# Row sums of two head pairs in four column tiles, a later normalisation and projection, and four PSUM banks at both ends

## What is computed

```
x = x + 0.5 * ffn(layernorm(x))
x = x + attention_block(layernorm(x))
x = x + 0.5 * ffn(layernorm(x))
```

```
attn = softmax(q k^T / 8)
y = (attn v) w_proj + b_proj + z
y = (y - mean) / sqrt(var + 1e-6) * gamma + beta
```

## Time and profile before

| what | value |
|---|---|
| median of 3 runs | 2347.0 us (2346.77 to 2348.1) |
| the profiled execution | 2348.62 us |
| its span, first to last instruction | 2346.8 us |
| TensorE busy | 2217.9 us, 95% |
| VectorE busy | 1670.9 us, 71% |
| ScalarE busy | 1194.5 us, 51% |
| GpSimd busy | 1470.6 us, 63% |
| mean granted TensorE clock | 0.98 of full speed |

### The profile page before, as it was taken

One profiled execution on the slowest core, in us unless ns is written; L12 is line 12 of the kernel. 1 busy time (PEld: TensorE's weight loads), 2 busy tenths in 40 slices (PEclk: granted clock), 3 DMA queues, 4 the chain that ended last, 5 costly groups with the idle time before them and its releaser, 6 DMA issues.

```text
span 2346.8 us, 38775 instructions
## 1 busy us (share of the span) xinstructions
PE 2217.9 (95%) x14537; PEld 1120.2 (48%) x14537; DVE 1670.9 (71%) x2734; ACT 1194.5 (51%) x1813; POOL 1470.6 (63%) x1419
## 2 busy tenths in 40 slices
PE   3799999999999999999999999999999999999983
PEld 1344445545454554545555454555545454454541
DVE  4465778777787777778777777877777787776643
ACT  1345554545555465555546555554555555454531
POOL 2266666766676675667667576766757676575642
PEclk9799999999999999999999999999999999999985
DMA  1000000000000000000000000000000000000000
GB/s 53 5 7 2 2 7 2 11 2 11 2 7 7 2 11 2 11 2 7 6 2 11 2 11 2 7 7 2 11 2 11 2 6 6 2 7 2 7 2 9
DMA packets 167495, 15.85 MB, mean 7 GB/s; under 512 B 148304, under 2 KB 166928, under 8 KB 167312
## 3 DMA queue, kind: packets, MB, share of 16 engines
q1 hardware_dynamic: 167312, 13.39, 4.9%
HBM read 7.03 MB, written 4.19 MB: 5 GB/s over the span
## 4 chain that ended last, share of the span: by engine, by line
PE 82%; DVE 12%; issue 4%; POOL 1%; ACT 1%; DMA 0%; SPq 0%; POOLq 0%
PE pS L920 21%; PE pO L947 18%; PE pM L904 9%; PE pX L932 6%; PE pX L968 5%; PE pM L1066 5%; DVE nmax L769 3%; PE pM L957 3%; PE FpF L248 2%; PE LpF L283 2%; PE FpF L283 2%; PE LpF L259 2%; PE LpF L248 2%; PE FpF L259 2%; DVE ON L863 1%
## 5 line engine op out<-in xcount | busy, mean ns | idle before, releaser
L634 POOL TENSOR_TENSOR ES<-ES,E 128x512 f32<-128x512 f32 x512 | 701.2, 1390 | 212.6 <-ACT E L721 210.2
L721 ACT ACTIVATE E<-pS 128x1024 f32<-128x1024 f32 x512 | 522.9, 1021 | 411.9 <-PE pS L920 407.6
L769 DVE TENSOR_REDUCE nmax<-pX 128x2 fp32r<-128x1024 f32 x512 | 621.9, 1215 | 129.3 <-PE pX L932 126.4
L947 PE MATMUL pO<-E,VA 128*64 128x512 f32 x2048 | 552.3, 618 | 0.0
L628 POOL TENSOR_TENSOR ES<-E 128x512 f32<-128x512 f32 x256 | 321.4, 1276 | 260.9 <-ACT E L721 260.6
L904 PE MATMUL pM<-xf,w_raw 128*64 128x512 f32 x1024 | 266.1, 598 | 3.1 <-DVE QL L872 2.4
L932 PE MATMUL pX<-KH,QH 64*128 64x512 f32 x1024 | 249.5, 426 | 7.7 <-DVE nmax L769 5.0
L920 PE MATMUL pS<-QH,KH 64*128 64x512 f32 x1024 | 255.5, 496 | 0.0
L920 PEld LDWEIGHTS pS<-QH,KH 64*128 64x128 f32 x1024 | 95.4, 183 | 253.3 <-issue 252.0
L932 PEld LDWEIGHTS pX<-KH,QH 64*128 64x128 f32 x1024 | 189.7, 306 | 51.3 <-DVE nmax L769 12.4
L920 PE MATMUL pS<-SH,onesr 64*128 64x512 f32 x1024 | 203.3, 393 | 0.0
(11 more groups left out here) (135 smaller groups left out, 3291.2 us busy)
## 6 DMA issues: line engine op xcount, KB each, us to landing
RROW<-RC SPq DMA_DIRECT2D x512, 2.0 KB, 2.0
xin<-in_L_attn_x SPq DMA_DIRECT2D x16, 256.0 KB, 3.0
SH<-nmax SPq DMA_DIRECT2D x256, 2.0 KB, 2.0
LC<-LROW SPq DMA_DIRECT2D x256, 2.0 KB, 2.1
out<-X SPq DMA_DIRECT2D x16, 256.0 KB, 2.5
w_raw<-in_L_attn_w_q SPq DMA_DIRECT2D x1, 512.0 KB, 4.7
w_raw<-in_L_attn_w_k SPq DMA_DIRECT2D x1, 512.0 KB, 5.5
w_raw<-in_L_attn_w_v SPq DMA_DIRECT2D x1, 512.0 KB, 6.7
```

The lines of the kernel that those rows point to most:

```text
L634: ins = g.tensor_tensor(ES[par][:, hd, :], ES[par][:, hd, :], E[s][:, hd, :], ALU.add)
L721: a.activation(E[s][:, :, :], pS[:, :, :], ACT.Exp).then_inc(s_exp, 1)
L769: v.tensor_reduce(nmax[px % 2][:, :, t:t + 1], pX[:, :, :], AX.X, ALU.max, negate=True).then_inc(s_max, 1)
L947: ins = pe_.matmul(pO[half(hd), :], VA[of][:, kt, j * 128 + 64 * hd:j * 128 + 64 * hd + 64], E[kt][:, hd, :], start=kt == 0, stop=kt == KT ...
```

## The change

1. Row sums. They are made for two pairs at once, at step 2 of every second pair, at the end of that step on TensorE: four groups of matmuls with 32 columns of ones each, into the four quarters of the partitions of `pM`. `ES` gets a third buffer. `LROW`, `LC`, `REC`, `RC` and `RROW` each carry two pairs: one copy, four DMAs, one reciprocal, two small operations and eight DMAs for two pairs.
2. The broadcast and `ON` come for pair `i-3`, the projection for pair `i-4`.
3. The pieces of `L` move: transposes of x 28, gate 29 to 0, up 1 to 4, transposes of h 10, 11, 13, 14, down 15; on VectorE maxima of h in 4 and 6, rounding of h in 8 and 11, moments of y in 14 and of x2 in 18, maxima of x in 22, rounding of x in 26. `X1` gets three and `X2` two buffers. The pieces of `F` stay, but for one addition on GpSimd (L571), from step 23 to step 25.
4. Both ends. For block 0 of `F` and block 15 of `L` the four row tiles use four banks (`pF`, `pO`, `pM` and half of `pS`), so that a gate needn't wait for the one before it. The first layer norm and quantisation of x stand beside the quantisation of the weights, before the loop, and the loop starts at block -1. Two of the first rounds of V move to block -1, the third to block 0. For block 15 the multiplication by gamma and the addition behind it are on VectorE.

```diff
+    def apart(self, c):
+        return c == self.alone
+    def bank(self, c, k):
+        return self.spare[k] if self.apart(c) else self.pF
...
         if k == 0:
             pe.wait_ge(self.s_xqT, c + 1)
-        else:
+        elif not self.apart(c):
             pe.wait_ge(self.s_silu, 4 * c + k)
...
-        for b in range(-2, B + 2):
+        for b in range(-1, B + 2):
...
-                    if there(i - 2, NP):
-                        sp.wait_ge(s_rlo, i - 1)
-                        for hl in range(2):
-                            for hd in range(2):
-                                sp.dma_start(RROW[2 * hl + hd:2 * hl + hd + 1, :].bitcast(F32),
-                                             RC[old][:, hl, hd, :].bitcast(F32)).then_inc(s_rrow, 16)
+                    if p % 2 == 1 and there(i - 2, NP):
+                        sp.wait_ge(s_rlo, i // 2)
+                        for j in range(4):
+                            for hl in range(2):
+                                r = 4 * hl + j
+                                sp.dma_start(RROW[r:r + 1, :].bitcast(F32), RC[:, hl, j, :].bitcast(F32)).then_inc(s_rrow, 16)
...
-                        if t == 15:
+                        if t == 18:
                             dve.wait_ge(s_x2, c + 1)
-                            norm_x2.moments(nc, dve, c, X2)
-                        if t == 19:
+                            norm_x2.moments(nc, dve, c, X2[c % 2])
+                        if t == 22:
                             dve.wait_ge(norm_x2.s_out, c + 1)
                             L.dve_max_x(dve, c)
-                        if t == 22:
+                        if t == 26:
                             L.dve_round_x(dve, c)
...
-                        if s == 3 and there(i - 2, NP):
-                            dve.wait_ge(s_rb, i - 1)
-                            wait(dve, s_proj, i - 2)
-                            v.tensor_tensor(ON[:, :], OT[(p - 2) % 4][:, :], pM[:, :], ALU.mult).then_inc(s_norm, 1)
+                        if s == 3 and there(i - 3, NP):
+                            dve.wait_ge(s_rb, i - 2)
+                            wait(dve, s_proj, i - 3)
+                            v.tensor_tensor(ON[:, :], OT[(p - 3) % 4][:, :], pM[:, :], ALU.mult).then_inc(s_norm, 1)
...
-                def row_sums(i, par):
-
-                    pe.wait_ge(s_add, 3 * i + 3)
-                    wait(pe, s_norm, i - 1)
-                    pe.wait_ge(s_klo, min(i + 4, NP) if isinstance(i, int) else i + 4)
-                    for hd in range(2):
-                        ins = pe_.matmul(pM[half(hd), :], ones[:, 0:64], ES[par][:, hd, :], start=True, stop=True)
+                def row_sums(i):
+
+                    pe.wait_ge(s_add, 3 * i)
+                    wait(pe, s_norm, min(i - 3, NP))
+                    pe.wait_ge(s_klo, min(i + 3, NP))
+                    for j in range(2):
+                        for hd in range(2):
+                            r = 32 * (2 * j + hd)
+                            ins = pe_.matmul(pM[r:r + 32, :], ones[:, 0:32], ES[(i - 2 + j) % 3][:, hd, :], start=True, stop=True)
                     ins.then_inc(s_l, 1)
...
-                        if s == 2 and there(i - 1, NP):
-                            row_sums(i - 1, 1 - p % 2)
                         first_ffn(b, 4 * p + s, bpar)
                         last_ffn(b, 4 * p + s, bpar)
-                        if s == 1 and there(i - 3, NP):
+                        if s == 1 and there(i - 4, NP):
                             project(i, p)
+                        if s == 2 and p % 2 == 0 and there(i - 1, NP):
+                            row_sums(i)
```

More of the change, by code:

```diff
@@ L419, in make_program @@
         E = [m.sb(f"E{kt}", [128, 2, S]) for kt in range(KT)]
-        ES = [m.sb(f"ES{i}", [128, 2, S]) for i in range(2)]
+        ES = [m.sb(f"ES{i}", [128, 2, S]) for i in range(3)]
         OT = [m.sb(f"OT{i}", [128, S]) for i in range(4)]
@@ L525, in body @@
                                          nmax[new][:, hd, :].bitcast(F32)).then_inc(s_sh, 16)
-                    if p == 4 and there(b + 2, B) and there(b + 1, B):
+                    if p == 4 and there(b + 2, B):
                         sp.wait_ge(s_x1, b + 2)
[L528 to L531, removed]
-                        for hd in range(2):
-                            sp.dma_start(LC[new][:, hd, :], LROW[64 * hd:64 * hd + 1, :]).then_inc(s_lc, 16)
+                        sp.dma_start(tiles(xin[:, :]), x_g[b + 2]).then_inc(s_x, 16)
+                    if p == 4 and there(b - 2, B):
+                        sp.wait_ge(s_res, b - 1)
+                        sp.dma_start(out_g[b - 2], tiles(X2[b % 2][:, :])).then_inc(s_out, 16)
+                    if p % 2 == 0 and there(i - 1, NP):
+                        sp.wait_ge(s_lrow, i // 2)
+                        for j in range(4):
+                            sp.dma_start(LC[:, j, :], LROW[32 * j:32 * j + 1, :]).then_inc(s_lc, 16)
                 steps(sp, body)
@@ L1023, in body @@
                             scores(i, p, s)
-                        if s == 3 and there(i - 2, NP):
-                            pe.wait_ge(s_rrow, 64 * (i - 1))
-                            pe.wait_ge(s_lrow, min(i, NP) if isinstance(i, int) else i)
-                            wait(pe, s_norm, i - 2)
-                            pe_.matmul(pM[:, :], sel[0:64, :], RROW[0:64, :], start=True, stop=True).then_inc(s_rb, 1)
+                        if s == 3 and there(i - 3, NP):
+                            pe.wait_ge(s_rrow, 128 * ((i - 1) // 2))
+                            pe.wait_ge(s_lrow, min(i, NP) // 2)
+                            pe.wait_ge(s_klo, min(i + 3, NP))
+                            wait(pe, s_norm, i - 3)
+                            pe_.matmul(pM[:, :], sel[0:64, (i - 3) % 2, :], RROW[0:64, :], start=True, stop=True).then_inc(s_rb, 1)
                         if s < 2:
@@ new lines, in body @@
+                        if s == 2 and p % 2 == 0 and there(i - 1, NP):
+                            row_sums(i)
+                        for r in rounds_at(i, s):
+                            kt, of, xb = round_place(i, p, bpar, r)
+                            pe.wait_ge(s_klo, min(i + 3, NP))
+                            wait(pe, s_va, r)
+                            if there(i - 3, NP):
+                                pe.wait_ge(s_norm, i - 2)
+                            elif i == 2:
+                                pe.wait_ge(s_lrow, 1)
+                            if p == 5:
+                                pe.wait_ge(s_xf, b + 2)
+                            for n in range(2):
+                                ins = pe_.matmul(pM[half(n), :], xf[xb][:, kt * 128 + 64 * n:kt * 128 + 64 * n + 64],
+                                                 w_raw[:, 2, of * S:of * S + S], start=True, stop=True)
+                            ins.then_inc(s_v, 1)
```

298 lines of the change are left out of this document (150 added, 148 removed).

## The result

The change made the kernel slower: median 2422.1 us (2420.9 to 2423.3) against 2347.6 us (2346.8 to 2350.4) for the kernel before on the same chip, ratio 1.0315 with an interval of 1.0299 to 1.0332. The forecast was 2360 with a range of 2300 to 2405: the sign is right, the size is wrong by 62 us, and the time lies outside the range. The profiled execution took 2423.3 us, its span is 2421.4 us.

What follows compares the result with a forecast made beforehand. TensorE was taken to bound the middle 14 blocks. From the profiled 2348.6 us, row sums -46.7, moved pieces +84, start -19 and end -4 gave 2363, or 2361 against the median; the forecast was 2360, range 2300 to 2405.

Steps and rivals of the forecast that it cites:

- row sums: TensorE's sums: 64 fewer at 0.86 us, less 8.3 us for changes of matmul form; 46.7 us less.
- step 26 to 27: Both roundings of x in step 26 delay ON; step 27's V round stalls 2.3 us in 13 blocks, 30 us.
- step 18 to 19: Moments of x1 and x2 ahead of ON; step 19's V round stalls 2.4 us in 14 blocks, 34 us.
- step 22 to 23: L's maxima of x in step 22 delay ON; the V round stalls 1.0 us in 14 blocks, 14 us.
- steps 7 to 12: VectorE's maxima and roundings of h for F and L: 0.9 us of stall in 13 blocks, 12 us.
- start: Before the first scores: earlier norm, four banks, two V rounds moved; 19 us less (bounds 12 and 23).
- end: Last block: four banks save 8.0 us, a longer broadcast chain costs 3 to 5; 4 us less in sum.
- What bounds, and the V round: TensorE bounds the middle 14 blocks; the V round, 2.52 us after a step's first score matmul, stalls if ON is late.
- A: Rival: VectorE is not late, stalls of 20 us in all, time 2291; chance 0.34 (below 2342).
- B: Rival: no change, losses meet gains with stalls of 5.2 to 6.0 us a block, 2342 to 2352; chance 0.13.
- C: Rival: four tiles of 32 columns run two by two, row sums save nothing, 2415; chance 0.09.
- D: Rival: the broadcast waits for RROW, 0.5 us for each of 64 doubles, 32 us more, 2393; chance 0.04.

Runs made afterwards that it cites:

- the filler: The changed kernel with four unused products of 64 columns (1.7 us) added ahead of the V round in steps 19 and 27: 2391.3 us.
- other places of the pieces: Changed kernel with x2's moments, F's rounding and both maxima of x later: 2304.2 us; with L's first maxima of h in step 3, second rounding in 15: 2287.1.
- the first way to place L's rounding: The 2304.2 us version with L's first maxima of h in step 3, roundings of h in 7 and 15 instead of 8 and 11: 2305.6 us.

## Why the prediction was wrong

Term by term, by the steps of the prediction. The measured column has the mean wait of a step in the mature blocks times 14 blocks, where a wait is meant (that of step 27 comes in 13).

| term | predicted | measured |
|---|---|---|
| row sums | -46.7 | -46: a double costs 0.14 more, a single one less 0.86, 64 of each |
| step 26 to 27 | +30 | +30 (2.17 us) |
| step 18 to 19 | +34 | +32 (2.30 us) |
| step 22 to 23 | +14 | +20 (1.41 us) |
| steps 7 to 12 | +12 | +38: 3.14 us in steps 7, 9, 11 and, behind the roundings of 11 and 12, 13, less 0.42 before |
| stalls of before that go | -6 | -7 (0.13 and 0.36 us in steps 25 and 27) |
| half clock behind the waits | not there | +31 |
| start | -19 | -18.2 |
| end | -4 | -1.5 |

The measured terms add up to 78; the spans differ by 74.6.

**What bounds, and the V round: right.** The waits for `ON` came in the three steps named, 81.2 us in all (3 of them in step 11) for 78 forecast. In steps 19 and 27 the numbers taken were 2.4 and 2.3 us, inside bounds of 1.3 to 3.4 and 2.1 to 3.0, so that they came out as close as 0.1 is in part luck. A step's TensorE work, VectorE's work left over from the step before, and the 2.52 us to the V round gave each of them to half a microsecond.

**The step that failed: "Steps 7 to 12", 0.9 us a block, where 2.7 were measured.** It was worked out as a balance, 28.5 us of VectorE's work against 23.9 of TensorE's with 3.5 of slack, while the three other places were followed instruction by instruction. A balance has no order in it. The order says that the projection of step 9 or 13 wants `pX`, which the row maxima of the same step must have left, and that these stand behind a rounding from the step before: L's of 1.8 us in step 8, F's of 2.9 us in step 12, which itself is late by L's of 3.5 us in step 11. The waits of steps 9 and 13 (0.94 and 1.29) come by this. That of step 7 (0.77) comes by F's product with its bank, which stands behind L's maxima of step 6 and `ON`. Cutting L's rounding of h took 24 us away from the attention part.

**The term that was missing: the clock.** I priced a wait at its own length. Of those of 2.2 to 2.3 us in steps 19 and 27, 20 were followed by 3.41 us at half clock (the 21st stretch of the attention part is in block 0), and the filler, which removes the gaps without removing any work or lateness of VectorE, gave 31 us back, some 1.5 us for each. The Trainium skill has the rule that an idle TensorE falls back to 1.2 GHz ("TensorE: Matmul & The Clock Gate", part 1, the HAM clock gate), and the granted clock of 0.50 behind these waits agrees. The trace of before, with a wait of 1.94 us and no such stretch in its attention part, had given me no reason to price it. With these two terms the prediction's own sum of 2361 would have been 2361 + 26 + 31 = 2418, within 4 us of the measured time; the errors of the other terms are small and partly cancel.

**The start: right.** The first gate came at 21.90 us, as forecast, and from it to the end of the last up product are 9.6 us, where the prediction had 10.4.

**The end: half right.** With the ends alone the tail is 10.9 us shorter. Four banks are 8.9 of these (gate to last up product takes 9.5 us for 18.45 before), where the prediction had 8.0; the rest stands ahead of the gate, where two operations moved to VectorE; for them and an earlier norm of y it had 3. The lengthening of the chain to the last broadcast, put at 3 to 5 us, is 9.6 us: 29.0 behind the last step's start against 19.5 before (2276.76 in the earlier trace rows, the step began at 2257.29). That takes back nearly all of it.

**L's moved steps as a whole: 129 us and not 84**, by the run that has them alone. With the row sums added the attention part falls by 34.9 us only (2289.5 to 2254.6), not by 46.7, though two half clock stretches fewer are in it: steps 6, 14, 22 and 30 lose 0.86 us each, and steps 7 and 23 win 0.79 and 0.85 of it back as longer waits, because VectorE is as late as it was. The waits of steps 19 and 27 became 0.14 shorter each. Work taken out of TensorE just ahead of a wait for VectorE is not gained.

**Rivals.** A (VectorE is not late) is refuted for the kernel as it stands; its 2291 is near what other places of the pieces gave (2304.2, 2287.1), but there the lateness was moved away and wasn't absent. B (losses meet gains) is refuted: the stalls were larger than forecast and not smaller. C is refuted by the 0.86 us of a double. D is refuted: no mature block waits for RROW. The 5.7 us of such waits, where the prediction had set 5 as the limit, are one in block 0 and one in the tail. One number of the rivals is wrong by itself: with half of the 90 us of stalls the time is 2316, and 2319 is the sum with half of the 84.

## What to carry to other kernels

Where several engines run a fixed list of steps, follow the order of the busiest helper through every step in which two of its pieces meet, and ask of each task of the bounding engine which buffer it overwrites and who must have left that buffer; a sum over several steps hides exactly these waits. Price a wait of TensorE of some 2 us with the slower clock that may follow it, and when one can't be removed, try work of no use in its place. A change that brings its saving together with a new schedule should be run with each part alone: here the ends were worth 29.5 us and the row sums 21 to 31 (21 by the spans with L's later steps, 2442.1 and 2421.4, which come from different chips, 31 by the ratios), and the schedule beside them cost 129 in the attention part until its pieces had been placed again.

## What the runs showed of the hardware

- In the kernel after the granted clock was 0.5 for 3.41 us behind all 13 waits of TensorE of 2.17 us in step 27, behind 7 of 14 waits of 2.30 us in step 19, and once in block 0. With x2's moments moved it was so behind 5 of 13 waits of 2.17 us. Waits of 1.4 us and less in the mature blocks were never followed by it; one of 1.84 us in step 8 was, in one block of the first way to place L's rounding. In block 0 waits of 1.66 to 2.19 us were followed by it in most variants, and the wait of 1.94 us before was not. With 1.7 us of dummy matmuls in the gaps of steps 19 and 27 no stretch was left there.
- Four column tiles of 32 with 512 columns each in float32 take 0.86 us, the same as two tiles of 64. A step with them is 0.14 us longer than one with the sums of one pair in tiles of 64 (3.82 for 3.68 us in step 18).
- A VectorE operation of 0.16 us took 1.24 us when a GpSimd addition (1.24 us each) had begun 0.04 us ahead of it. With 0.86 us more of TensorE work in step 18, the addition came 0.21 us behind it, and `ON` was 1.1 us earlier against the step's start.
